# A two-layer recurrent block: rope rounded a tile later, two small loads issued earlier, no counting events in attention

## The reference, cut to what matters

```python
q = (x @ Wq.T) ...; k = (x @ Wk.T) ...; v = (x @ Wv.T) ...      # 32 query heads, 8 key heads, 16 wide
q = q * cos + _rotate_half(q) * sin                              # "rope"
k = k * cos + _rotate_half(k) * sin
scores = jnp.where(causal, q @ k.T / sqrt(16), min)
attn = softmax(scores); s = (attn @ v) @ Wo.T
w_gu = _dequant(qweight_gu, ...); w_d = _dequant(qweight_down, ...)   # 4-bit weights, scales, zeros
h = silu(gate) * up;  ffn = h @ w_d
```

## Time and profile before

| | us |
|---|---|
| median of 3 runs | 1494.02 |
| the runs | 1491.23, 1497.5, 1494.02 |
| profiled execution, its time | 1493.29 |
| its span | 1491.6 |
| busy in the span: PE | 1350.5 (91%) |
| DVE | 1063.0 (71%) |
| ACT | 619.0 (41%) |
| POOL | 334.7 (22%) |

### The profile page before, as it was taken

One profiled execution on the slowest core, in us unless ns is written; L12 is line 12 of the kernel. 1 busy time (PEld: TensorE's weight loads), 2 busy tenths in 40 slices (PEclk: granted clock), 3 DMA queues, 4 the chain that ended last, 5 costly groups with the idle time before them and its releaser, 6 DMA issues.

```text
span 1491.6 us, 20742 instructions
## 1 busy us (share of the span) xinstructions
PE 1350.5 (91%) x6642; PEld 928.8 (62%) x6642; DVE 1063.0 (71%) x2495; ACT 619.0 (41%) x859; POOL 334.7 (22%) x387
## 2 busy tenths in 40 slices
PE   3788998982988699999999997999999999999998
PEld 2566776761766577777777764555555555555467
DVE  6887977774777455555554576888888888888547
ACT  4643755442432111111111110566666666666662
POOL 2653567441322000000000000222212222212221
PEclk9978998985999899999999995999999999999999
DMA  6111200005333100000100050111112132221002
GB/s 217 54 36 49 85 0 29 0 29 182 109 120 110 61 21 22 22 24 20 36 8 16 5 96 1 33 33 33 33 38 58 36 90 61 62 62 33 2 29 85
DMA packets 45171, 76.15 MB, mean 51 GB/s; under 512 B 9556, under 2 KB 16804, under 8 KB 45076
## 3 DMA queue, kind: packets, MB, share of 16 engines
q1 hardware_dynamic: 43086, 73.36, 17.8%
q10 hardware_dynamic: 1990, 1.62, 0.4%
HBM read 55.67 MB, written 19.01 MB: 50 GB/s over the span
## 4 chain that ended last, share of the span: by engine, by line
PE 61%; DVE 6%; issue 3%; ACT 2%; DVEq 1%; ACTq 1%; DMA 0%; POOL 0%; POOLq 0%; SPq 0%
PE d_bank L1827 12%; PE d_bank L37 10%; PE d_bank L1867 9%; PE d_bank L39 9%; PE d_bank L38 9%; PE d_bank L1851 9%; DVE d_bank L1586 1%; PE d_bank L1875 1%; DVE mx_first L1589 1%; DVEq L1592 1%; PE d_bank L1696 1%; DVE hl L1449 0%; DVE hs L1446 0%; DVE ql L1558 0%; ACT hh L1348 0%
## 5 line engine op out<-in xcount | busy, mean ns | idle before, releaser
L1384 ACT ACTIVATE prob<-d_bank 128x1024 f32<-128x1024 f32 (+3 forms) x384 | 303.2, 811 | 220.5 <-PE d_bank L1851 216.4
L1586 DVE CUSTOM_DVE_ANT_0 d_bank<-d_bank,mask 128x128 f32<-128x128 f32 (+3 forms) x512 | 247.4, 503 | 61.1 <-PE d_bank L1827 54.9
L1827 PE MATMUL d_bank<-kst,qst 96*128 96x512 f32 (+3 forms) x768 | 268.5, 390 | 6.2 <-DVE mx_first L1589 3.1
L1827 PEld LDWEIGHTS d_bank<-kst,qst 96*128 96x128 f32 x768 | 145.5, 193 | 154.0 <-DVE mx L1586 56.4
L1851 PE MATMUL d_bank<-qst,kst 98*128 98x512 f32 (+3 forms) x768 | 210.5, 357 | 0.5 <-ACT prob L1384 0.5
L1249 POOL TENSOR_SCALAR_AFFINE_SELECT prob<-prob 128x256 f32<-128x256 f32 x256 | 104.4, 408 | 458.3 <-ACT prob L1384 456.8
L1589 DVE TENSOR_REDUCE mx_first<-d_bank 128x1 f32<-128x512 f32 x256 | 176.2, 688 | 17.8 <-PE d_bank L1827 13.1
L1867 PE MATMUL d_bank<-prob,vst 128*32 128x512 f32 (+3 forms) x1536 | 164.5, 500 | 1.2 <-POOL prob L1249 1.2
L1340 ACT ACTIVATE hs<-d_bank 128x512 f32<-128x512 f32 (+1 forms) x44 | 26.3, 598 | 311.7 <-PE d_bank L39 311.7
L37 PE MATMUL d_bank<-xtl,wgh 128*128 (+1 forms) x352 | 141.2, 401 | 11.2 <-DMA zz<-z_gu_scr 11.2
L1851 PEld LDWEIGHTS d_bank<-qst,kst 98*128 98x128 f32 x768 | 129.7, 191 | 18.7 <-ACT prob L1384 8.2
(11 more groups left out here) (256 smaller groups left out, 2429.2 us busy)
## 6 DMA issues: line engine op xcount, KB each, us to landing
wst<-L_ffn_w SPq DMA_DIRECT2D x8, 1024.0 KB, 6.6
qst<-q_scr SPq DMA_DIRECT2D x32, 256.0 KB, 4.6
qw<-L_ffn_qweight_gu SPq DMA_DIRECT2D x40, 128.0 KB, 2.6
xb<-L_attn_x SPq DMA_DIRECT2D x4, 1024.0 KB, 6.7
x_d<-xb SPq DMA_DIRECT2D x4, 1024.0 KB, 4.3
xb<-x_d SPq DMA_DIRECT2D x4, 1024.0 KB, 6.4
q_scr<-qh SPq DMA_DIRECT2D x16, 256.0 KB
q_scr<-ql SPq DMA_DIRECT2D x16, 256.0 KB
```

Source lines behind the costliest of these rows:

```text
L1384: act.activation(prob[:, c // 2 % 2, c % 2 * 2:c % 2 * 2 + 2, lo:], score_bank[c % 2][:, :, lo:], ACT.Exp, scale=D ** -0.5).then_inc(exp_d ...
L1586: dve.tensor_tensor_reduce(sc, sc, mask[:, CH - w:CH], 1.0, LEAST, ALU.add, ALU.max, mx[:, u, h % 2, h // 2, q:q + 1]).then_inc(spare_free, 1)
L1827: pe.matmul(spare_bank(number)[:, 0:w], qst[u][0:M_ROW, h // 2, q * P:q * P + P], kst[u][0:M_ROW, h % 2, at:at + w], start=True, stop=True ...
```

## The change

It does three things. (1) ScalarE rounds rope tile r-1 where it rounded tile r, and VectorE makes `ql` of tile r-1 after the sum of tile r; both do the last tile after the loop. Piece 4 is made after tile 1 of the last chunk and piece 5 after tile 3 (before: tiles 2 and 4), their rows are broadcast after tiles 2 and 4 (before: 3 and 5), and piece 4 uses banks 0 and 1, which have become free there. (2) SP issues the scales of step 1 right behind the last store, ahead of the wait for the last stores to land; later steps wait for one step less; TensorE waits for them in front of the first piece and no longer at the start of the body. (3) The counting events in front of masked maxima and of masks go.

```diff
-        MADE = {(1, 2): 0, (2, 0): 1, (2, 2): 2, (3, 0): 3, (3, 2): 4, (3, 4): 5}
-        ROWS = {(1, 2): 0, (2, 1): 1, (2, 3): 2, (3, 1): 3, (3, 3): 4, (3, 5): 5}
+        MADE = {(1, 2): 0, (2, 0): 1, (2, 2): 2, (3, 0): 3, (3, 1): 4, (3, 3): 5}
+        ROWS = {(1, 2): 0, (2, 1): 1, (2, 3): 2, (3, 1): 3, (3, 2): 4, (3, 4): 5}
...
+        def row_banks(s, b, n):
+            if s == 0:
+                return (0, 1) if (b, n) == (1, 1) else (6, 7)
+            return 2 * (n % 2), 2 * (n % 2) + 1
...
             def scales(s):
-                if s > 0:
-                    sp.wait_ge(w_ready, 6 * s + 1)
+                if s > 1:
+                    sp.wait_ge(w_ready, 6 * (s - 1) + 1)
...
+            scales(1)
             for r in range(CHUNKS * ROT - HALVES + 1, CHUNKS * ROT):
                 stored(r)
             for s in range(LAST):
-                scales(s + 1)
+                if s > 0:
+                    scales(s + 1)
...
-                        pool.sem_inc(diag_seen, 1)
...
-                    if m >= 1:
-                        round_rope(c, m - 1)
+                    if m >= 1 and c * ROT + m >= 2:
+                        round_rope(c * ROT + m - 2)
...
+            round_rope(CHUNKS * ROT - 1)
             act.wait_ge(q_free, CHUNKS * ROT)
...
+            def low_rope(r):
+                dve.wait_ge(qh_ready, r + 1)
+                dve.tensor_tensor(ql[:, r % HALVES], qc[:, r % 2], qh[:, r % HALVES].bitcast(F32), ALU.subtract).then_inc(ql_ready, 1)
...
-                    dve.wait_ge(qh_ready, r + 1)
-                    dve.tensor_tensor(ql[:, r % HALVES], qc[:, r % 2], ...).then_inc(ql_ready, 1)
+                    if r > 0:
+                        low_rope(r - 1)
...
+            low_rope(CHUNKS * ROT - 1)
             values(CHUNKS - 1)
...
                 if at + w == (q + 1) * P:
-                    dve.sem_inc(item_seen, 1)
...
-                pe.wait_ge(w_ready, number + (1 if n == 0 or s == 0 else 0))
+                pe.wait_ge(w_ready, number + (1 if n == 0 or s == 0 and number < 4 else 0))
+                if s == 0 and number == 4:
+                    pe.wait_ge(v_ready, CHUNKS)
...
             def body(s, b):
-                pe.wait_ge(sz_in, 32 * (s + 2))
                 gate_up(s, b, 0, 0)
                 def first_piece():
                     pe.wait_ge(h_ready, tile(s, b, 0, 0) + 3)
+                    pe.wait_ge(sz_in, 32 * (s + 2))
                     piece(s + 1, b, *PIECES[0])
```

More of the change, by code:

```diff
@@ L963, in layer1 @@
         const_in, cleared = sem("const_in"), sem("cleared")
-        item_seen, diag_seen = sem("item_seen"), sem("diag_seen")
         qk_in = [sem(f"qk_in{u}") for u in range(STACKS)]
@@ L989, in rope @@
             return c * ROT + k
-        def row_banks(s, n):
-            return (6, 7) if s == 0 else (2 * (n % 2), 2 * (n % 2) + 1)
+        def row_banks(s, b, n):
+            if s == 0:
+                return (0, 1) if (b, n) == (1, 1) else (6, 7)
+            return 2 * (n % 2), 2 * (n % 2) + 1
         def piece_number(s, b, n):
@@ L1307, in _, with round_rope @@
             high_parts(0, range(TPC))
-            def round_rope(c, k):
-                r = rope(c, k)
+            def round_rope(r):
                 act.wait_ge(rope_ready, r + 3)
@@ L1428, in piece @@
                     src, into = qw[:, 0], [flat(a[s % 2][:, k])[0:rows] for a in (wdh, wdl)]
-                scale_bank, zero_bank = (v3(bank[:, k]) for k in row_banks(s, n))
+                scale_bank, zero_bank = (v3(bank[:, k]) for k in row_banks(s, b, n))
                 dve.tensor_scalar(v3(wq[:, :]), v3(src), lane_shift[0:rows, 0:1], 15, ALU.logical_shift_right,
@@ L1556, in _ @@
                     dve.tensor_tensor(qc[:, r % 2], bank[:, 4 + r % 2], qc[:, r % 2], ALU.add).then_inc(rope_ready, 1)
-                    dve.wait_ge(qh_ready, r + 1)
-                    dve.tensor_tensor(ql[:, r % HALVES], qc[:, r % 2], qh[:, r % HALVES].bitcast(F32), ALU.subtract).then_inc(ql_ready, 1)
+                    if r > 0:
+                        low_rope(r - 1)
                     if c + 1 < CHUNKS and m in (1, 3):
@@ L1690, in piece @@
                 number = piece_number(s, b, n)
-                scale_bank, zero_bank = (bank[:, k] for k in row_banks(s, n))
+                scale_bank, zero_bank = (bank[:, k] for k in row_banks(s, b, n))
                 pe.wait_ge(hot_ready, number + 1)
-                pe.wait_ge(w_ready, number + (1 if n == 0 or s == 0 else 0))
+                pe.wait_ge(w_ready, number + (1 if n == 0 or s == 0 and number < 4 else 0))
+                if s == 0 and number == 4:
+                    pe.wait_ge(v_ready, CHUNKS)
                 if kind == "gu":
```

## The result

The changed kernel takes 1472.68 us in the median of 4 runs (1469.95 to 1473.26), the one before 1493.92 on the same chip (4 runs, 1491.23 to 1497.5): ratio 0.9857, 95% interval 0.9833 to 0.9881, 21.2 us faster. Forecast were 12.1 us and 1481.9.

The account below looks back on a forecast made before the run. TensorE was taken to bound attention, while in projection and rope TensorE and VectorE hold each other up. Scales 4.8, rope 4.5, events 2.0 + 0.8 make 12.1 us off 1494.02, giving 1481.9; range 1475 to 1490.

Parts of the forecast that it names:

- rival C: Attention: maxima earlier by 0.15 us in mid-group let TensorE load weights earlier; 9 us for the events, 1475.7 us, chance 0.15.
- part 3: Removing the counting events: 2.0 us at group ends plus 0.8 in the maxima ahead of the first group, masks 0.
- 15 x 0.13 at the group ends: Attention: one event per group end on the path, 0.13 us without work before a masked maximum, 2.0 us in all.
- if groups get over 0.5 us shorter: Attention: a sign that the prediction is wrong; a group was expected to get 0.1 to 0.2 us shorter.
- 6.3 us of stands at the group ends: Attention: TensorE's whole stand for VectorE, at the ends of 15 groups, taken as the most the groups could gain.
- The 0.15 us per event: VectorE's start behind a matmul's end: 0.19 us with the event between, 0.04 without, for 118 starts that really waited.
- I had said 4.0: Projection and rope: the last chunk starts at 455.9 instead of 459.9, by two leads of 2.0 and 2.1 us.
- the load of piece 5: Last chunk: a new stand of 1.3 us for packed weights, loaded behind a later store while the piece is made earlier.
- The ring at the last rounding: End of rope: ScalarE may round tile 19 only when SP has passed tile 18's stores, a stand of 2.0 us.
- the clock held at the start of the last chunk: Last chunk's first product: with less idle time ahead TensorE keeps the higher clock, 1.6 us more gained.
- my upper end of 8.6: Rope: the most it could gain, with no new stands, 4.5 + 4.1 us.
- the hop from the values to the matmul: Start of feed-forward: 0.1 us for the semaphore between the copy of the last values and TensorE's first matmul.

Follow-up runs that it names:

- the run with load and ring: Changed kernel with piece 5's packed weights loaded one tile earlier and SP's wait for tile 16's store put ahead of tile 18's stores: 1466.16 us, ratio 0.9821.

## Why the prediction was wrong

The direction was right and the size fell short: 21.2 us against 12.1, outside my range of 1475 to 1490 and below even the 1475.7 of rival C.

**The failed step** is in part 3 and in the first paragraph: "TensorE bounds it, and what VectorE saves is idle time unless TensorE stood for it, which it did for 6.3 us". I took TensorE's busy time as work. It holds waits: 8.24 us of it went away with no matmul less. So 2.0 us (15 x 0.13 at the group ends) became 7.8, and in the run without VectorE's events 8.1. The last maxima of a group, on which I put everything, are worth 0 by the run with events there alone. Three places in the midst of a group, which I left out, and its first maximum, just behind the combining, are worth all of it: 0.52 us a group, and "if groups get over 0.5 us shorter" was one of my signs of being wrong. VectorE and TensorE pass three banks to and fro there, and where TensorE's next matmul waits for the bank, a bank handed back late is a later matmul. That is close to the mechanism of rival C, maxima that pass their 0.15 us on in the midst of a group. That C's size fits too, 9 for part 3 against 8.1 + 0.8 = 8.9, is luck: it was made of 6.3 us of stands at the group ends, which did not shrink. What I held against C, "TensorE was idle only 10.6 us in 495", was the same misreading. The 0.15 us per event itself was right, but of the 118 starts of maxima that waited only three per group count, and the first of a group besides.

The Trainium skill (Perfetto Trace Analysis, sections Sequencer-only Instruction and DVE / Act Engine Instruction) has the sequencer wait for the semaphores of a sequencer-only instruction before it can fetch the next one, while a VectorE instruction that carries its wait is put in a wait queue and leaves the sequencer free. This agrees with the run that has the events behind the operation (groups 475.49 us) and with the one that has them in front of the reductions (478.87). The rule of the Trainium skill (VectorE: DVE Perf Modes, section Rules for kernel authors) to minimise the count of operations and not the semaphores does not hold for an event that takes the wait: taking 512 of them away gave 11.3 us, and they hold no operation.

**Rope: mechanism right, two sizes off.** Counted from the first projection matmul the last chunk started 8.2 us earlier (84.24 to 76.01), and I had said 4.0. Tile by tile the lead arises at four places: 1.35 us in the first tile, 1.5 in front of the fourth tile of the second chunk (0.7 of them a shorter wait of TensorE for the rows of piece 0), and 1.6 and 3.8 at the two stands for `xtl`, which fell by 5.3 together. The 1.35 us are the clock and not rope's own: before ran its first tile at a granted clock of 0.65, after at 1.00. It does not reach the end of the stage, for where a kernel of the new order ran its first tile at the lower clock too (the runs with events behind the maxima and in all items but the last 8), the fourth tile of the second chunk took 3.0 us at the higher clock and not 4.6, and the values end at 111.0 and 111.1 all the same. Only the run with events in the last 8 items ran both tiles slowly, and its values end at 114.09. The other profiles with the pieces at their new places and the load as it was have 111.1 to 111.5. Then the load of piece 5 took back 3.98 where I had 1.3; I had let it leave a store later but not reckoned that it takes 5.37 us to land. The ring at the last rounding was 2.04 for my 2.0, and the clock held at the start of the last chunk as I expected (2.9 us for the first product). In sum 6.7 for 4.5; with neither stand it would have been 12.7 by the run with load and ring, more than my upper end of 8.6.

**The scales: right.** 4.35 us for 4.8; the term that was off is the hop from the values to the matmul, for which I had put 0.1 without a row and which took 0.57. The first silu did not come later by the stores: 491.02 - 483.68 = 7.3 us after the start, where it was 7.2. What I did not see is that the two parts need each other: 3.1 and 4.3 alone, 11.0 together, since each term of my sum was taken with the other already done.

**The masks of GpSimd:** 0, right, with a run of its own (groups 483.72 against 483.69).

In all: forecast 4.8 + 4.5 + 2.8 = 12.1; measured in the profiles 4.35 + 6.7 + 8.55 = 19.6, and in the timed runs 21.2. VectorE's events alone gave 11.3 us in timed runs and 8.9 in the profile, and the interval allows both. **Open:** the 1.5 us between the 19.7 of the table and the timed 21.2, which executions of one kernel differ by anyway. And no run put the event in front of one of the four maxima alone; that they are the four is read from the traces and agrees with the runs on parts of the group.

## What to carry to other kernels

A wait belongs on the operation that needs it and not on an instruction put in front: free in a place with slack, it cost 8 us where two engines exchange few buffers. Do not read a full TensorE as one that never waits: its matmuls' records overlap, and a short wait can lie hidden under the neighbour's record. Look for matmuls that start right behind the hand-back of their bank, and price an earlier hand-back by these and not by the stands shown. And when work is moved forward, move its load and the store that frees its buffer too: here they gave back 6 of 12.7 us, and a few changed lines brought them home in that stage (1466.16 us in all).

## What the runs showed of the hardware

- An increment on VectorE that takes the wait in front of an operation delays it by 0.15 us (0.19 us behind the matmul's end for 0.04; the kernel after has 0.04 at the same maxima); the same increment behind the operation costs nothing measurable (groups 475.49 us with it and 475.89 without).
- The profile's busy time of TensorE is not its work alone: the same 2975 matmuls showed 474.86 us busy or 466.62. A wait for a bank can be covered by the neighbour's record: the matmul of item 24 began 0.34 us behind the start of the one in front in before and 0.18 in after, each time some 0.06 us after its bank came back, with 0.01 us of idle time shown at most. That the whole 8.24 us are such waits is not shown one by one.
- The packed load of piece 5 (256 KB) took 5.37 us from issue to landing, issued right behind two stores of rope; the last store took 5.0 to 5.1.
- Executions of the same instructions differ in place: the second layer's projection began at 370 to 379 us in the profiles, and its second tile came 2.8, 4.2 or 5.3 us behind that, at granted clocks of 1.00, 0.65 and 0.50, while four profiles of the groups with all events lie within 0.6 us of each other and the five without any in the kernels like the one after within 1.2.
